# A routing stage in eight rounds: three steps moved one round later, and a new order of steps on each engine

## What is computed

```
x = _layernorm(x + attention(x))                       # attention ends with  out @ Wo
gating = softmax(x @ Wg + bg)                          # 8 logits for each token
top_k_indices = argsort(gating)[..., -2:]              # the best two experts
h = silu((x @ W1 + b1) * (x @ W3 + b3))                # for the chosen experts
mixed = sum(topk_w * (h @ W2 + b2))
x = _layernorm(x + mixed @ Wf + bf)
```

## Time and profile before

| | |
|---|---|
| median of 3 executions | 1900.16 us (1898.84 to 1901.07) |
| the profiled execution | 1903.75 us, span 1902.1 us |
| TensorE busy | 1732.0 us, 91% of the span |
| VectorE busy | 1245.9 us, 66% |
| ScalarE busy | 896.5 us, 47% |
| GpSimd busy | 335.1 us, 18% |
| mean granted clock of TensorE | 0.950 |

### The profile page before, as it was taken

One profiled execution on the slowest core, in us unless ns is written; L12 is line 12 of the kernel. 1 busy time (PEld: TensorE's weight loads), 2 busy tenths in 40 slices (PEclk: granted clock), 3 DMA queues, 4 the chain that ended last, 5 costly groups with the idle time before them and its releaser, 6 DMA issues.

```text
span 1902.1 us, 28295 instructions
## 1 busy us (share of the span) xinstructions
PE 1732.0 (91%) x9130; PEld 912.9 (48%) x9131; DVE 1245.9 (66%) x2992; ACT 896.5 (47%) x1042; POOL 335.1 (18%) x468
## 2 busy tenths in 40 slices
PE   6999889999999999999999999977549999999965
PEld 3544344444444444444444444246526666666644
DVE  3688876787788778777777777026535555555536
ACT  2876765555555555555555554635302222222236
POOL 0000021121211211111112111114561111111111
PEclk9999979999999999999999998987669999999988
DMA  3464446030110210201102112046421111111144
GB/s 106 163 236 166 154 142 231 7 106 9 42 66 7 75 40 10 98 7 46 63 7 80 35 39 91 7 125 224 153 79 46 47 48 44 44 44 44 50 130 155
DMA packets 99595, 155.32 MB, mean 82 GB/s; under 512 B 10880, under 2 KB 60832, under 8 KB 99104
## 3 DMA queue, kind: packets, MB, share of 16 engines
q1 hardware_dynamic: 85088, 122.57, 19.6%
q0 software_dynamic: 14400, 31.37, 4.7%
HBM read 87.90 MB, written 65.35 MB: 81 GB/s over the span
## 4 chain that ended last, share of the span: by engine, by line
PE 70%; DVE 5%; issue 5%; DMA 4%; ACT 4%; SPq 1%; POOL 0%; ACTq 0%; DVEq 0%; POOLq 0%
PE att_ps_s L1046 22%; PE exp_ps_h L1679 13%; PE att_ps_o L1065 13%; PE att_ps_m L268 10%; PE exp_ps_y L1697 6%; DMA att_sums<-att_out_t 3%; DVE att_maxima L278 2%; ACT att_probs L1093 2%; PE exp_ps_t L1687 2%; PE route_ps_g L1251 1%; PE exp_ps_x L1668 1%; PE route_ps_y L1251 1%; DVE fin_stats L1210 1%; PE fin_ps_y L1251 0%; DVE fin_res L1900 0%
## 5 line engine op out<-in xcount | busy, mean ns | idle before, releaser
L1093 ACT ACTIVATE att_probs<-att_ps_s 128x1024 f32<-128x1024 f32 (+3 forms) x640 | 562.5, 896 | 445.4 <-PE att_ps_s L1046 437.3
L1046 PE MATMUL att_ps_s<-att_queries,att_keys 49*128 49x512 f32 (+3 forms) x2560 | 618.6, 555 | 22.6 <-ACT att_probs L1093 17.1
L278 DVE TENSOR_REDUCE att_maxima<-att_ps_m 128x1 f32<-128x512 f32 x768 | 487.2, 684 | 125.8 <-PE att_ps_m L268 121.5
L268 PE MATMUL att_ps_m<-att_keys,att_queries 48*128 48x512 f32 (+3 forms) x1280 | 480.6, 580 | 22.0 <-DVE att_maxima L278 11.7
L268 PEld LDWEIGHTS att_ps_m<-att_keys,att_queries 48*128 48x128 f32 x1280 | 191.3, 187 | 310.4 <-DVE att_maxima L278 159.7
L1046 PEld LDWEIGHTS att_ps_s<-att_queries,att_keys 49*128 49x128 f32 x2560 | 238.9, 190 | 143.2 <-ACT att_probs L1093 100.8
L281 DVE CUSTOM_DVE_ANT_0 att_ps_m<-att_ps_m,att_future 128x128 f32<-128x128 f32 (+3 forms) x512 | 241.4, 513 | 67.8 <-PE att_ps_m L268 66.8
L1065 PE MATMUL att_ps_o<-att_probs,att_values 128*32 128x512 f32 (+3 forms) x2560 | 270.8, 541 | 0.7 <-POOL att_probs L1149 0.7
L1679 PE MATMUL exp_ps_h<-keep_w,exp_rows_t 128*128 x568 | 258.3, 598 | 5.7 <-DVE exp_rows_t L1713 5.7
L1755 ACT ACTIVATE exp_hidden<-exp_product 128x512 f32<-128x512 f32 x71 | 44.8, 632 | 344.2 <-DVE exp_product L1738 344.2
L1149 POOL TENSOR_SCALAR_AFFINE_SELECT att_probs<-att_probs 128x512 f32<-128x512 f32 x128 | 83.5, 653 | 454.6 <-ACT att_probs L1093 454.5
(11 more groups left out here) (179 smaller groups left out, 1430.3 us busy)
## 6 DMA issues: line engine op xcount, KB each, us to landing
att_queries<-q_parts SPq DMA_DIRECT2D x64, 192.0 KB
att_keys<-k_parts SPq DMA_DIRECT2D x64, 192.0 KB
exp_rows<-sorted_rows SPq DMA_DIRECT2D x71, 129.0 KB, 2.3
v_rows<-pre_v_sb SPq DMA_DIRECT2D x8, 1024.0 KB, 4.5
q_parts<-pre_waves SPq DMA_DIRECT2D x16, 512.0 KB, 5.4
k_parts<-pre_waves SPq DMA_DIRECT2D x16, 512.0 KB, 6.1
att_values<-v_rows SPq DMA_DIRECT2D x32, 256.0 KB
out_parts<-att_out_t POOLq DMA_DIRECT2D x32, 256.0 KB, 5.9
```

The costliest lines, as they stand in the source:

```text
L268: pe.matmul(bank[:, 0:width], self.queries[g % 2][half, c, r, P * q:P * q + P], self.keys[g % 2][half, k, r, 0:width], start=True, stop=Tr ...
L278: dve.tensor_reduce(to, bank[:, 0:width], AX.X, ALU.max).then_inc(self.s_mr, 1)
L1046: mm = pe.matmul(score_tile(unit, first, last)[:, e], keys[g % 2][half, k // TPC, r, P * (k % TPC):P * (k % TPC) + P].bitcast(F32), querie ...
L1093: act.activation(probs[:, step % PROBS, DUO * r:DUO * r + DUO, first:last], score_tile(unit, first, last), ACT.Exp, scale=SCALE).then_inc( ...
```

## The change

The three pipelines get other lags and another order. `shift_logits`, `exponential` and `choose` go from lag 2 to lag 3, `count_before` and `give_places` from 3 to 4. On TensorE `count_before` now comes ahead of `turn_x1`; on ScalarE `exponential` ahead of `keep_x1_t`; on VectorE `shift_logits` stands right behind `scale_and_shift`, ahead of `residual` and `divide`. The steps themselves are the same. ScalarE's list now has a deepest lag of 3 and is written out without a loop, by `pipelined`'s own rule.

```diff
@@ block.tensor
-            pipelined(pe, NCH, [(project, 1), (turn_x1, 2), (count_before, 3), (project_gates, 2)])
+            pipelined(pe, NCH, [(project, 1), (count_before, 4), (turn_x1, 2), (project_gates, 2)])
@@ block.scalar
             pipelined(act, NCH, [
                 (normalise, 2),
+                (exponential, 3),
                 (keep_x1_t, 2),
-                (lambda i, p: norm.root(act, i, eps[:, 0:1]), 1),
-                (exponential, 2)])
+                (lambda i, p: norm.root(act, i, eps[:, 0:1]), 1)])
@@ block.vector
-            pipelined(dve, NCH, [(scale_and_shift, 2), (residual, 1), (divide, 0), (last_inverses, 0), (shift_logits, 2),
-                                 (give_places, 3), (choose, 2)])
+            pipelined(dve, NCH, [(scale_and_shift, 2), (shift_logits, 3), (residual, 1), (divide, 0), (last_inverses, 0),
+                                 (give_places, 4), (choose, 3)])
```

## The result

The change made the kernel slower: 1909.89 us median (17 runs, 1902.11 to 1922.32) beside 1901.29 us (17 runs, 1895.21 to 1907.80) for the kernel before on the same chip, a ratio of 1.005 [1.0029, 1.0071]. The profiled execution took 1904.79 us, with a span of 1903.1 us.

A forecast was written before the change was run, and what follows sets the result against it. GpSimd's 64 puts, kept waiting by rounds that form a ring over three engines, end the stage. Rounds of 11.7 us, then five unbroken chunks of puts, end it 8.3 us earlier: 1900.16 becomes 1891.9 us, range 1885.3 to 1897.0.

The forecast's parts named there:

- The end of project of chunk 3: On TensorE: project of chunk 3 takes 5.4 us and ends at 1296.1; the shorter rounds count from there.
- VectorE's parts: VectorE's steps in one routing round, back to back, from scale_and_shift to residual with its statistics: 9.9 us.
- The ring of 11.7 us: Routing rounds: project, count_before, turn_x1 to project_gates' start, and project_gates on TensorE form the longest ring, 11.7 us a round.
- Count_before, now ahead of turn_x1, … adds no wait: TensorE's queue: count_before waits for choose, which is over before normalise begins, so it costs only its own 0.5 us.
- the forecast gain: End of routing: the last put ends at 1389.1 instead of 1397.5, 8.3 us less.
- From there GpSimd is never idle: GpSimd's puts from chunk 3's places at 1338.2: five chunks without a pause, 50.9 us, ending at 1389.1.
- Puts of 0.96 us, 1.27 apart: GpSimd: each put lasts 0.96 us and costs 1.27 us back to back, a chunk of eight 10.14 us.
- my slower rival: GpSimd's puts stretched by a denser VectorE: 0.56 us more on each of 40 puts, 1914.3 us; chance 0.06.
- They don't decide: Second path into the experts: zeros in SyncE's queue end near 1381, tables near 1373, before the last put.
- Loads and clock: Divide's loads 1 to 3 us late, TensorE's clock mixed as before; rival of cold clock or late loads, chance 0.17.

The follow-up runs named there:

- f1: The changed kernel with GpSimd starting its puts only after the last chunk's places, so none run beside the rounds; 1941.80 us beside 1897.51, one run.
- g3: The changed kernel with a small memset behind each put, setting puts 1.46 us apart instead of 1.27; 1898.49 us beside 1902.03, one run.
- k1: The changed kernel with a 0.33 us memset behind each put, all chunks spaced, timed in full; ratio 1.0011 to the kernel before.
- k2: The changed kernel with a memset behind each put in the first five chunks only; ratio 1.0022 to the kernel before.
- e3: The kernel before with one edit: count_before, same lag, moved ahead of turn_x1 on TensorE; ratio 1.0109, 1921.32 us beside 1899.89.
- e1: The changed kernel with count_before put back behind turn_x1 on TensorE, lags as in the change; ratio 1.0024 to the kernel before.
- e2: The changed kernel with count_before behind project_gates, last in TensorE's list; ratio 1.0045 to the kernel before.
- g2: The changed kernel, count_before behind turn_x1, GpSimd pausing before each chunk's sixth put until the next chunk's count has signalled; ratio 1.0013 to the kernel before.
- k4: The changed kernel with puts of the first five chunks spaced and the 2 MB of bias loaded behind chunk 7's loads; ratio 1.0017 to the kernel before.
- g1: The changed kernel with GpSimd pausing before each chunk's sixth put until turn_x1 and the counts have signalled; ratio 0.9999 to the kernel before.
- g4: The kernel before with each chunk's counts made by 6 wider matmuls instead of 14; ratio 0.9991.
- f2: The kernel before with all puts delayed until after the last chunk's places; 1961.59 us beside 1897.51, one run.
- k3: The kernel before with the puts of its first five chunks spaced 1.46 us apart; ratio 0.9993.
- e4: The changed kernel with each chunk's counts made by 6 wider matmuls instead of 14; ratio 1.0036 to the kernel before.
- f3: The changed kernel with count_before behind turn_x1 on TensorE and give_places behind choose on VectorE; ratio 1.0075 to the kernel before.

## Why the prediction was wrong

I gave 1891.9 us, 0.83 for faster and 0.06 for slower. It is slower by 0.5%, outside the range.

- **The end of project of chunk 3: right.** I had 1296.1, which is +38.4. It ended at 1289.80, +38.4. The first places and the first put came where that puts them.
- **VectorE's parts: right.** I summed 9.9 us a round; the undisturbed one took 9.4. The wait at L1500 did vanish from the rounds without a hold.
- **The ring of 11.7 us: right as a mechanism, not as a result.** Without puts beside them (f1) rounds take 10.3 to 11.1 us where no load is late; with spaced puts 12.6 on average in g3, 12.7 in k1, 13.0 in k2. In after, the projects of chunks 3 and 7 end at 1289.80 and 1347.94, 14.5 us a round, by the same count more than the 13.9 of before.
- **"Count_before, now ahead of turn_x1, … adds no wait": this step failed.** I asked only when its input was ready and costed it at 0.5 us. Behind this lies a term that I put at nothing without a reason: that every signal of TensorE goes up when its matmuls end. In after, turn_x1's come up to 4.68 us late and the logits' 8.86 and 5.97, and VectorE stands still for 10.49 and 12.40 us at L1500. e3 puts a price on the place alone, in the kernel before: 17.7 us of the stage. It is not the whole: with the place put right (e1) about half of the loss goes, and the forecast gain does not come, because VectorE then waits for the late counts themselves. I had a row for every duration of TensorE but read none of its signals against the end of the work; count_before's, 4.5 to 5.1 us late in five rounds, were in the trace of before.
- **"From there GpSimd is never idle": failed in consequence.** I had chunk 3's puts at 1338.2 (+80.5) and the last five chunks without a pause, ending at +131.4. They began at +86.7, 6.2 us later, and had two pauses of 4.60 and 4.75 us instead of 0.30. That is 6.2 + 4.3 + 4.4 = 14.9 us, and the last put indeed ended at +146.3. The first pause is behind project of chunk 7, the second behind VectorE's 12.40 us at the last shift_logits: give_places of chunk 6 now stands behind it. I had not costed this place in the queue at all.
- **Puts of 0.96 us, 1.27 apart: right**, with two exceptions, of 1.96 and 1.52 us. For that rival I read the one long put of before as standing beside VectorE's widest operations; two more of these, of the same width, at 1383.41 and 1384.20, stood beside puts of 0.96 us. So my slower rival, puts stretched by VectorE, is not what happened: it had the right two parties, GpSimd's puts and a busier round, and the wrong victim.
- **"They don't decide", on zeros and tables: held in after, but barely.** I had the zeros' end 8 us ahead of the last put's; it was 0.7 us ahead (1397.10 and 1397.77). The zeros ended last, by more than 5 us, in e2, g2, k2 and k4, and by 1 to 3 us in e1, g1 and g4. I took 12.88 us as their own length, but it goes from 8.6 to 23.7 us.
- **Loads and clock**: in after divide waited for no loads. It waited 4.86 us in e1, 3.54 in f1 and 5.73 in g2, more than the 1 to 3 us I had allowed for chunk 7. The clock of the stretches shown was 0.77, as before (0.76).

**What stays open** is what in the chip holds the increments. It needs puts beside it (f1, f2) and is as a rule smaller when they are 1.46 us apart (k3, g3, k1), though not always (k2). It shows first behind count_before in the kernel before, but not because of the number of its matmuls (e4, g4). Counts in fp32 instead of bf16 were not tried, nor a kernel without count_before, so whether its burst starts the hold or only meets it is argued, not shown. Every execution on record has a span and a granted clock beside its time, so all were recorded by the profiler; whether the signals are late without it no run shows. Nor is it settled that the held signals need a pause: in before each came 1.5 to 2.3 us behind a chunk's last put, but in after and e3 some came while puts ran. What makes the zeros long is open too.

## What to carry to other kernels

When a step is moved, read for the steps around it how long after their last instruction the semaphore went up and what else ran then, not only how long they take: a late signal can be hidden by the old order and laid bare by the new. A wait in the profile that names no engine although the producer ended long ago was the sign here. Where an engine issues indirect DMAs back to back, a faster ring beside it can remove the pauses in which held signals came through, so test the gain once with those DMAs out of the way and once with them spaced.

## What I had not expected of the hardware

- TensorE's semaphore increments came up to 15.2 us late (f3) beside indirect DMAs issued from GpSimd 1.27 us apart. At 1.46 us apart the largest lateness in the rounds was 2.7 us in g3, 5.7 in k1 and 8.1 in k2, without such DMAs 0.01 us (f1, f2).
- TensorE's own stream was stretched too: in after single 8-column matmuls of a count start after 0.54 and 1.25 us of idle time, at 1316.60 and 1318.02, and the count ends 3.1 us after project, where in f1 it ends 0.3 us after it. VectorE, in the same kernel and beside the same puts, made its dependent steps without a stop (1298.45 to 1307.89).
- SyncE's eight small DMAs behind one another took 8.6 us beside spaced puts (g3, k1) and anything from 9.7 us (f1) to 23.7 us (k4) beside dense ones. What makes this difference is open.
